# Unit 0's queries loaded into the query weight columns, and more of its row maxima placed among the last local tiles

## The reference

```python
# local: RMS norm and rotary on q and k, 4 key heads for 16 query heads, causal within 64 tokens
scores = einsum('bhqd,bhkd->bhqk', q, k) * scale
mask = causal | local
attn = softmax(where(mask, -10000, scores));  local_out = (attn @ v) @ Wo.T + bo
# routed: a gate picks, per token, one head's k and v, shared by all 16 query heads
indicator = one_hot(argmax(softmax(x @ W_gate.T)))
k_shared = einsum('bth,bthd->btd', indicator, k);  v_shared = einsum(..., gating_top1, v)
att = softmax(causal(einsum('bhqd,bkd->bhqk', q, k_shared) / sqrt(32)));  y = att @ v_shared
return x + local_out + y
```

## Time and profile before

| | |
|---|---|
| median of three runs | 713.08 us (711.9 to 714.23) |
| the profiled execution | 714.07 us, its span 712.8 us |
| mean granted clock of TensorE | 0.963 |
| PE busy | 661.3 us, 93% |
| DVE, ACT, POOL busy | 499.6, 364.4, 440.8 us |
| transfers | 55.05 MB, mean 77 GB/s |

### The profile page before, as it was taken

The page is one execution under the profiler, slowest core; times in us unless marked ns, Lnnn a source line. Parts: engine busy times, 40 slices in busy tenths (PEclk is TensorE's granted clock), DMA queues, the critical chain, the costliest instruction groups (busy, mean ns, idle before and its releaser), DMA issues.

```text
span 712.8 us, 19481 instructions
## 1 busy us (share of the span) xinstructions
PE 661.3 (93%) x7433; PEld 519.1 (73%) x7433; DVE 499.6 (70%) x1345; ACT 364.4 (51%) x907; POOL 440.8 (62%) x366
## 2 busy tenths in 40 slices
PE   4689999999999999999977899799999999999997
PEld 3477778888788888787866477567777777777775
DVE  3956767656776675667645879777879797978544
ACT  5445435654255563365442056155666565656674
POOL 2965676944766736695821058267877777877740
PEclk9989999999999999999997779789999999999999
DMA  8513212231221322212135310310404040323011
GB/s 294 186 57 90 66 57 71 74 94 58 79 64 56 105 72 64 67 58 74 49 109 158 90 47 25 84 46 26 127 28 127 27 127 26 104 51 83 5 32 33
DMA packets 64014, 55.05 MB, mean 77 GB/s; under 512 B 6320, under 2 KB 48688, under 8 KB 63920
## 3 DMA queue, kind: packets, MB, share of 16 engines
q1 hardware_dynamic: 61760, 52.87, 25.2%
q10 hardware_dynamic: 2160, 0.93, 0.5%
HBM read 35.63 MB, written 17.89 MB: 75 GB/s over the span
## 4 chain that ended last, share of the span: by engine, by line
PE 75%; DVE 7%; POOL 5%; ACT 5%; DMA 3%; issue 3%; SPq 1%; ACTq 0%; DVEq 0%; POOLq 0%
PE gemm L896 15%; PE s_ps L1014 12%; PE st_ps L1045 11%; PE od_ps L1059 11%; PE gemm L982 5%; PE od_ps L1073 5%; PE gemm L892 3%; ACT p_loc L1447 3%; PE win L956 3%; PE s_ps L1083 2%; PE win L941 2%; DMA rope_t<-rope 2%; POOL rms_y L1556 2%; DVE l_sum L1230 2%; PE av L968 2%
## 5 line engine op out<-in xcount | busy, mean ns | idle before, releaser
L896 PE MATMUL gemm<-w_tok,xt 128*128 128x512 f32 (+1 forms) x768 | 184.7, 383 | 4.6 <-DVE g_exp L1144 1.8
L1280 DVE CUSTOM_DVE_ANT_0 s_ps<-s_ps,x_ln 128x512 f32<-128x512 f32 (+3 forms) x236 | 135.5, 625 | 31.6 <-PE s_ps L1014 30.7
L896 PEld LDWEIGHTS gemm<-w_tok,xt 128*128 128x128 f32 x768 | 130.0, 192 | 28.2 <-DVE g_exp L1144 2.3
L1014 PE MATMUL s_ps<-k_stack,w_tok 96*128 96x512 f32 (+2 forms) x360 | 116.9, 407 | 2.3 <-DVE w_tok L1291 1.0
L1045 PE MATMUL st_ps<-w_tok,k_stack 98*128 98x512 f32 x288 | 103.9, 427 | 3.1 <-DMA w_tok<-w_tok 2.8
L1494 ACT ACTIVATE p_loc<-st_ps 128x512 f32<-128x512 f32 x144 | 77.5, 601 | 53.6 <-PE st_ps L1045 52.8
L1014 PEld LDWEIGHTS s_ps<-k_stack,w_tok 96*128 96x128 f32 x360 | 63.2, 198 | 34.9 <-DVE picked_fk L1280 15.8
L1280 DVE CUSTOM_DVE_ANT_0 s_ps<-s_ps,x_ln,picked_fk 128x256 f32<-128x256 f32 (+3 forms) x124 | 63.5, 562 | 10.7 <-PE s_ps L1014 10.5
L1447 ACT ACTIVATE p_loc<-win,l_max 128x96 f32<-128x96 f32 x256 | 61.0, 392 | 12.7 <-DVE l_max L1221 12.5
L1604 POOL TENSOR_TENSOR p_loc<-p_loc,l_rec 128x1536 f32<-128x1536 f32 x16 | 44.1, 2757 | 32.2 <-DVE l_rec L1233 32.0
L892 PE MATMUL gemm<-xt,w_qt 128*128 128x256 f32 x384 | 55.2, 291 | 8.9 <-DVE picked_fv L1175 5.2
(11 more groups left out here) (169 smaller groups left out, 1276.9 us busy)
## 6 DMA issues: line engine op xcount, KB each, us to landing
w_tok<-q_parts SPq DMA_DIRECT2D x96, 128.0 KB, 2.6
q_parts<-qt SPq DMA_DIRECT2D x128, 64.0 KB
x_ln<-x SPq DMA_DIRECT2D x8, 512.0 KB, 4.6
x_res<-x SPq DMA_DIRECT2D x16, 256.0 KB, 3.4
partial<-x_res SPq DMA_DIRECT2D x16, 256.0 KB, 2.0
k_t<-partial SPq DMA_DIRECT2D x8, 512.0 KB, 6.0
raw<-w_tok SPq DMA_DIRECT2D x3, 1024.0 KB, 12.7
v_win<-v_rows SPq DMA_DIRECT2D x64, 48.0 KB, 2.2
```

The source lines that it names most:

```text
L896: i = e.matmul(g[:, 0:cols], xs[l][:, k, a * P:(a + 1) * P], w_tok_p[r][:, k, c0:c0 + cols], start=first, stop=last)
L1014: e.matmul(s_ps[bank][:, 0:cols], q_op[b][0:HALVES, i, h, :], k_stack[0:HALVES, b * S + c0:b * S + c0 + cols], start=True, stop=True).then ...
L1280: e.tensor_tensor_reduce(out=s[:, 0:cols], in0=s[:, 0:cols], in1=causal[:, S - width + c0:S - width + c0 + cols], scale=1.0, scalar=dst if ...
```

## The change

Unit 0's queries no longer lie over the start of `w_tok0`, but in the 512 columns of the local query weights, four tiles of queries in each of `w_tok0` and `w_tok1`. These columns are free after the product (7, "q", 1), so all twelve loads are issued right after it, and `first_maxima` is added to the plan there instead of after the last product. Units 1 to 7 take their queries in turn in `w_qt` and `w_o`, made one tensor each. A row of maxima of unit 0 now goes out as four transfers of four heads' rows instead of one. `r_max` and `o_rec` are tensors of their own. While `gemm1` is in use every `first_max` step takes `tp1`; the alternation returns after it. The plan places 40 steps instead of 24 in the local stage. POOL builds the causal mask (`routed_rooms`) at the new place too.

```diff
@@ take_routed
-        if (n, kind, a) == (ROUNDS - 1, "fv", 1):
-            do("routed_rooms")
-            for quarter in range(2):
-                do("q_load", 0, 0, 0, quarter)
@@ take_q
+        if (n, a) == (ROUNDS - 1, 1):
+            do("routed_rooms")
+            for quarter in range(4):
+                do("q_load", 0, 0, 0, quarter)
+            p.add(routed, 4, background=True)
@@ take_qt
-        if (n, c) == (ROUNDS - 1, 1):
-            for quarter in range(2, 4):
-                do("q_load", 0, 0, 0, quarter)
...
-            p.add(routed, 1, background=True)
@@ first_maxima
-        while p.fk_stacked < ROUNDS - 1 or bank_free[1] is None or bank_free[1] > p.now:
-            yield None
...
-                    room = (("gemm", 1), "tp1")[t % 2]
+                    done = banks == [0] and bank_free[1] is not None and bank_free[1] <= p.now
+                    room = ("gemm", 1) if done and room == "tp1" else "tp1"
+                    p.turn["room", t] = room
...
-                    while p.free["V"] > p.now + 0.4:
+                    while p.free["V"] > p.now + 1.2:
                         yield None
-                    p.busy(p.now, ("V", 0.4 + cols / 960))
+                    p.busy(p.now + 0.1, ("V", 0.1 + cols * 0.00105))
...
-                yield 0.11, [("A", 0.27)]
                 do("max_low", 0, 0, 0)
-                yield 0, [("V", 0.35)]
+                yield 0.11, [("A", 0.27), ("V", 0.35)]
@@ rooms
-    w_rooms = [Room(t) for t in w_tok_p]
-    q_op = [room.piece(IT, HQ, P) for room in w_rooms]
+    q_later = [Room(t).piece(IT, HQ, P) for t in (w_o2, w_qt2)]
+    def q_op(u, i):
+        if u:
+            return q_later[u % B][:, i, :, :]
+        return w_tok_p[i // KC][:, i % KC, C_Q:C_Q + HD].rearrange("p (h q) -> p h q", h=HQ)
...
+    def load_rows(e, u, part, s, mark):
+        src = in_rows(u, part)[:, s, :].bitcast(F32)
+        if u:
...
+            return
+        for i in range(PART):
+            e.dma_start(q_op(0, part * PART + i)[HALVES + s:HALVES + s + 1, :, :].bitcast(F32),
+                        src[i * HQ:(i + 1) * HQ, :]).then_inc(*mark.did((u, part), inc=16))
@@ first_max on PE
-                lane.wait_ge(*M["fk_out"].of(ROUNDS - 1))
+                lane.wait_ge(*M["fk_out"].of(S // PAIR - 1))
@@ q_load on SP
-                    lane.wait_ge(*M["gemm_mm"].of((ROUNDS - 1, "fv", 1)))
+                    lane.wait_ge(*M["gemm_mm"].of((ROUNDS - 1, "q", 1)))
```

More of the change, by code:

```diff
@@ L714, in mixed_attention_kernel @@
     w_tok_p = [sb(one, f"w_tok{n}", [P, KC, W_COLS], F32R) for n in range(2)]
-    w_qt_p = [sb(one, f"w_qt{n}", [P, KC, HD], F32R) for n in range(2)]
-    w_o_p = [sb(one, f"w_o{n}", [P, KC, D], F32R) for n in range(2)]
+    w_qt2 = sb(one, "w_qt2", [P, 2, KC, HD], F32R)
+    w_o2 = sb(one, "w_o2", [P, 2, KC, D], F32R)
+    w_qt_p, w_o_p = ([w[:, n, :, :] for n in range(2)] for w in (w_qt2, w_o2))
     cos_t = sb(one, "cos_t", [P, S // P, 2, DK])
@@ L745, in mixed_attention_kernel @@
     warm = sb(one, "warm", [P, 1])
+    r_max = sb(one, "r_max", [P, IT, HQ])
+    o_rec = sb(one, "o_rec", [P, HQ])
     g_exp, g_score, g_hot = (sb(one, n, [P, 2, H]) for n in ("g_exp", "g_score", "g_hot"))
@@ L790, in piece @@
             return part.rearrange(f"p ({names}) -> p {names}", **dict(zip(names.split(), dims)))
-    w_rooms = [Room(t) for t in w_tok_p]
-    q_op = [room.piece(IT, HQ, P) for room in w_rooms]
-    r_max_t = w_rooms[0].piece(2, P, rows=HQ * IT)
-    r_first_t = [w_rooms[0].piece(2, P, rows=HQ * PART) for _ in range(2)]
+    q_later = [Room(t).piece(IT, HQ, P) for t in (w_o2, w_qt2)]
+    r_max_t, *r_first_t = (w_tok_p[0][0:HQ * n, kc, C_KVG:C_KVG + 2 * P].rearrange("p (s q) -> p s q", s=2)
+                           for kc, n in enumerate((IT, PART, PART)))
     causal = Room(x_ln).piece(S)
-    small = Room(picked["fk"])
-    r_max = small.piece(IT, HQ)
-    o_rec = small.piece(HQ)
     res = [k_t[:, b, HALF:HALF + S].rearrange("p (i c) -> p i c", i=IT) for b in range(B)]
@@ L819, in in_rows, with row_mark @@
         return r_max_t if u else r_first_t[part]
-    def rows_of(u, b, part, s):
-        i0, count = (0, IT) if u else (part * PART, PART)
-        return q_op[b][HALVES + s:HALVES + s + 1, i0:i0 + count, :, :].bitcast(F32)
+    def row_mark(name, part):
+        return M[name + "1" if part else name]
+    def load_rows(e, u, part, s, mark):
+        src = in_rows(u, part)[:, s, :].bitcast(F32)
+        if u:
+            e.dma_start(q_later[u % B][HALVES + s:HALVES + s + 1, :, :, :].bitcast(F32), src).then_inc(
+                *mark.did((u, part), inc=16))
+            return
+        for i in range(PART):
+            e.dma_start(q_op(0, part * PART + i)[HALVES + s:HALVES + s + 1, :, :].bitcast(F32),
+                        src[i * HQ:(i + 1) * HQ, :]).then_inc(*mark.did((u, part), inc=16))
     def turned_back(u, i):
@@ L1253, in vector_program @@
                 t, i, h, c0, cols = key
[L1254 removed]
+                s = first_room(t)
                 width = (i + 1) * P
                 dst = r_max[:, i, h:h + 1]
[L1257 to L1259 removed]
                 lane.wait_ge(*M["first_mm"].of(t))
@@ L1476, in scalar_program @@
                     lane.wait_ge(*M["rst_mm"].of((u - 2, len(PRODUCTS) - 1)))
-                e.dma_start(rows_of(u, b, part, 0), hi.bitcast(F32)).then_inc(
-                    *M["r_row"].did((u, part), inc=16))
+                load_rows(e, u, part, 0, row_mark("r_row", part))
             elif step == "routed_banks":
@@ L1735, in sync_program @@
                     lane.wait_ge(*M["rst_mm"].of((u - 2, len(PRODUCTS) - 1)))
-                e.dma_start(rows_of(u, b, part, 1), in_rows(u, part)[:, 1, :].bitcast(F32)).then_inc(*M["r_row_lo"].did((u, part), inc=16))
+                load_rows(e, u, part, 1, row_mark("r_row_lo", part))
             elif step == "q_load":
```

38 lines of the change are left out of this document (22 added, 16 removed).

## The result

The changed kernel takes 716.3 us (median of 20 runs, 710.7 to 719.9), the kernel before 712.9 (20 runs, 711.1 to 715.2): 1.0043 times as long, 95% interval 1.0028 to 1.0058. It is slower by 3.4 us, where 711.2 was forecast. The time lies inside the range, but the case that came is the second rival, to which the prediction gave 0.22 and 714.5 to 720, likeliest 717.

What follows compares the result with a forecast made beforehand. PE bounds the kernel: full-rate work plus 17.5 us waits and 17.8 lost at half clock, 35.3 together. After the change 16 + 6 + 4.2 + 6.7 + 0.5 = 33.4, 1.9 less: 711.2 us, range 703 to 719.

Steps and rivals of the forecast that it cites:

- second rival: Single bank thins PE so early that the clock falls at about 350; chance 0.22, 714.5 to 720, likeliest 717.
- The clock terms: Half-rate losses: 3 us from a fall before 387.6, 6.7 from one at the routed stage's start, clock low after 407.
- 3 more: Rest of the local stage: clock falls before 387.6, returns in about 9 us, partly hidden by DVE's pace; 3 us lost.
- Waits of the single bank, steps 0 to 14: From 342.3, steps sharing tp1 wait for copies and reductions: 3.8 us to 353, then 4.5 us.
- That the mask comes at no cost: Mask on POOL delays tile (7, 1)'s norm by 1.3 us, but its q_t waits for tp1 anyway: no cost.
- ACT's issues: Four transfers, 0.53 each, ahead of 16 exponentials at max_in_rows' first half: 2.1 us wait, two of 0.5 for banks.
- Waits up to 388: PE idle some 16 us between 342 and 388; forecast called wrong if under 10 or over 20 us.
- The start of the routed stage: Eight 512-column steps remain with max_in_rows right behind them on PE: 4.2 us of wait.
- The transition: Unit 0 to 1: low row earlier, wait 4.7 and fall 5.4 go, 0.5 left; 9.6 us removed.
- No instruction saved: Sixteen first_max steps replace row_scores steps with the same PE and DVE operations; PE's 92.2 us of work stay.
- The rule on the shared SBUF port pair: DVE's fk_lo of tile (7, 1) waits for POOL, holding up reductions by up to 1.5 us; sum then 712.7.
- The other rivals: Clock holds or is back at once: 0.2, 701.5, or 705 to 708 with one fall. Transition fails: 0.05, 721.

Runs made afterwards that it cites:

- mask_late: Changed kernel with DVE's wait for the causal mask moved to the first reduction of row maxima; 713.7 us, 1.0006 of the kernel before.
- sp_rows: Changed kernel with the four transfers of unit 0's high row, both halves, issued by SP instead of ACT; 711.9 us, 0.9988.
- mask_sp: Changed kernel with both edits, the mask wait moved (mask_late) and unit 0's high rows issued by SP (sp_rows); 711.4 us, 0.9985.
- early_tripled: mask_sp with each of the first 16 of unit 0's row-maxima products issued three times into the same place; 710.7 us, 0.9980.
- early_spaced: mask_sp with the planner made to wait until a step's bank is read before placing the next in it; 714.7 us, 1.0025.
- from_qt: mask_sp with unit 0's steps started at the first reading of a qt product (about 368), still in one bank until the products are done; 707.5 us, 0.9926.
- late_sp: late_fix with the wait for the mask back ahead of the bias of q of tile (7, 1), high row still on SP; 711.4 us, 0.9967.
- late_mask: late_fix with unit 0's high row issued by ACT again, the mask wait staying at the first reduction; 711.1 us, 0.9967.
- late_behind: late_fix with unit 1's low row held until unit 0's last output piece is added; 714.2 us, 1.0005.
- late_fix: mask_sp with the placement undone: unit 0's maxima start behind the last product, in two banks; queries' new place and early loads stay; 707.2 us, 0.9922.
- late_steps: Changed kernel with the placement alone undone: maxima behind the last product, in two banks, mask wait and ACT's issues kept; 713.0 us, 1.0004.
- late_again: Same text as late_fix, run again beside its neighbours on one chip; 708.0 us, 0.9918.
- late_one_bank: late_fix with all 32 of unit 0's early steps in the single bank tp1 instead of two banks; 726.0 us, 1.0180.

## Why the prediction went wrong, step by step

The case was decided by its second rival, and by the sign that this rival named, the clock of 348 to 356: it is at 0.50 from 352. Windows of the changed kernel:

```profile
341.30:388.00 46.70, 36.86 (x254) 27.64 (x252) 24.85 (x55) 15.16 (x50) 17.36 (x13) 0.80 0.20 56
...
345.00:352.00 7.00, 4.97 (x28) 3.15 (x26) 4.46 (x14) 3.05 (x8) 6.78 (x6) 1.00 0.24 55
352.00:356.00 4.00, 3.73 (x37) 3.07 (x41) 1.58 (x5) 0.21 (x1) 2.62 (x2) 0.51 0.08 28
356.00:362.25 6.25, 6.25 (x64) 4.89 (x61) 2.79 (x4) 2.72 (x11) 0.00 (x0) 0.50 0.32 100
```

and of the kernel before, which is full where the new order is thin:

```profile
345.00:352.00 7.00, 7.00 (x93) 5.84 (x95) 3.39 (x7) 2.89 (x7) 6.92 (x4) 1.00 0.37 105
```

- *The clock terms are the step that failed.* The forecast had two falls, "3 more" behind about 385 and 6.7 behind 407, 9.7 us together. There were six half-rate stretches and 21.2 us. The working took the thinning of 397 to 401 as the pattern that brings a fall, computed 3.9 us of work in the 7.5 from 345, and then put the first fall at 385; a fall at 350 it left to the rival. Measured is 4.97 us of work in the 7 from 345, less thin than computed, and the fall came. Five kernels with the steps at 343 fell between 348.5 and 353.25 in their profiles (the changed one, mask_late, sp_rows, mask_sp, early_tripled); the two that eased that stretch, early_spaced and from_qt, did not. What brings each of the five later falls is open.
- *Why the number was near all the same.* Two misses offset each other: the waits were forecast 4.9 us too high (23.7 against 18.8), the clock 11.5 too low. That 716.3 lies inside 703 to 719 is the width of the range and not the working.
- *Waits of the single bank, steps 0 to 14: 8.3 forecast.* Measured idle time from 341.3 to 380.8 is 6.9, of which 1.8 is the mask. The bank was mis-sized by about 3 us. From 352 on PE's own work at half rate lies between the steps and covers some of it; that was not in the forecast.
- *That the mask comes at no cost was wrong.* I followed the mask on POOL and missed that DVE's wait for it, in the step `routed_rooms`, had moved ahead of the bias. It cost 1.8 us by the trace, 2.5 by mask_late and 3.4 by late_sp.
- *ACT's issues: 2.1 and two of 0.5 forecast.* 2.95 by the trace (four took 3.15, not 2.1), and four more at 424.7 took 2.52 with unit 0's first exponentials behind them, which the forecast had not priced. 4.4 by sp_rows, 3.1 by late_mask.
- *Waits up to 388: 16 forecast, 9.8 measured* (341.3 to 388: PE busy 36.86 of 46.7). This too is under the 10 that the prediction named as its limit.
- *The start of the routed stage: right.* 4.2 us forecast, 3.4 measured in 417.8 to 427.9. Unit 0's first product came at 424.75, 13 us later than forecast, since PE had lost more at half rate ahead of it.
- *The transition: right.* 0.5 us of wait and no fall. late_behind prices it at 6.2 us (2.3 either way), where I had 9.6: the half rate that went with it was shorter in that kernel, 6.75 us against 13.7. The gain was oversized by some 3 us.
- *No instruction saved: right,* 329.4 and 329.3 us of work.
- *The rule on the shared SBUF port pair.* In the changed kernel `fk_lo` of tile (7, 1) took 0.86 us, against 0.17 for the one before it:

```profile
343.34 0.17 DVE L1205 TENSOR_TENSOR fk_stack<-chosen_fk,fk_stack 128x32 fp32r<-128x32 f32 x1
...
349.05 0.86 DVE L1205 TENSOR_TENSOR fk_stack<-chosen_fk,fk_stack 128x32 fp32r<-128x32 f32 x1
```

It ended at 349.91, when POOL's addition of 348.59 + 1.27 did. The Trainium skill, "SBUF — State Buffer", section "SBUF: two separate sides", has it that a VectorE operation with two SBUF inputs waits for a GpSimd one that reads SBUF and came first, for the whole of it. The trace agrees. The next reduction began 0.59 us behind the start of its product, the ones beside it 0.52 to 0.54, so the cost was under 0.1 us and not the 1.5 allowed for.

- *The other rivals.* The clock did not hold, and was not back at once: PE was busy 3.73 of 4 us from 352 to 356 and all of the 6.25 behind them, and the clock stayed at half rate until 362.25. The Trainium skill, "TensorE: Matmul & The Clock Gate", part 1, has it that activity releases the throttle. By that alone the prediction had about 706, and the rows above speak against it.

The whole 3.4 us, from the runs: the new places, eight more early steps and the early row of unit 1 win 5.8 (713.0 to 707.2, late_fix), the steps at 343 cost 4.2 (mask_sp), the mask's wait and ACT's issues together 4.8 (the changed kernel). That is +3.2, and it closes by construction, since each number is the step from one kernel to the next (713.0, 707.2, 711.4, 716.3). In the other order, waits kept and placement undone, late_steps is at 713.0, the time of the kernel before. Which half-rate stretch belongs to which of these is not settled: the stretches shift from run to run of one kernel.

## What to carry to other kernels

Work that one engine paces belongs where PE still has enough independent work between its steps; check the rate of PE's work in every few microseconds of the new order and ask of each thin place what the clock does, the first one above all. When a step is moved, follow each of its waits on each engine, and every DMA that it issues on an engine with urgent work behind it. A mended wait is worth its length plus or minus the half rate it brings, so mend and time them one by one and together: here 2.5 and 4.4 made 4.8, with 2 us of uncertainty. Compare two profiles from the point where the kernels part; and where the times of one kernel fall into groups, a profile speaks for its own group only.

## What the runs showed of the hardware

- A DMA issue on ACT took 0.51 to 0.60 us singly, but 0.79 and 0.63 each in rows of four (3.15 and 2.52 us), while SP issued four at about the same time in 2.62 and 2.65. An activation behind four such issues started 3.2 us late.
- One text's times spread by up to 1% with the mean clock (late_sp, 708.0 us at 0.972 to 714.8 at 0.960), and
  the clock fell and came back up to six times within 90 us, at places that differed between two executions of one text on two chips (late_fix and late_again). Ahead of the change, in the same work, one half-rate stretch lasted from 3.25 to 13.75 us.
- With PE busy 6.25 of 6.25 us (356 to 362.25, changed kernel) or 13.93 of 14 the clock stayed at 0.50; the lengths at half rate behind 342 run from 3.25 to 23.75 us (late_one_bank, 410.75 to 434.5).
